# Row transform of the first layer on sums and differences of columns w and w+256, with strips split on GpSimd

## The reference

```python
# layer 0: a 3x3 convolution with complex weights, in the frequency plane
X = jnp.fft.rfftn(x, axes=(-2, -1)); Xr, Xi = jnp.real(X), jnp.imag(X)
Yr = _rconv(Xr, wr) - _rconv(Xi, wi) + b_real[:, None, None]
Yi = _rconv(Xr, wi) + _rconv(Xi, wr) + b_imag[:, None, None]
y = jnp.fft.irfftn(lax.complex(Yr, Yi), axes=(-2, -1))
# layer 1: u, v = halves of the channels; whole rows are kept or set to zero
left_gate = relu(sign(einsum('bkmd,bkd->bkm', u, v.sum(axis=2))))[..., None]
y = concatenate([left_gate * u, right_gate * v], axis=1)
# layers 2 and 3: plain 3x3 convolutions, 16 to 16 channels, zero padding 1
```

## Time and profile before

| | |
|---|---|
| median of 3 runs | 4616.99 us (4616.7 to 4618.75) |
| the profiled execution, own time | 4618.31 us |
| its span | 4616.5 us |
| TensorE clock granted, mean | 0.959 of full speed |
| busy share: PE, PEld, DVE, ACT, POOL | 92%, 50%, 60%, 57%, 0% |

### The profile page before, as it was taken

One profiled execution on the slowest core, in us unless ns is written; L12 is line 12 of the kernel. 1 busy time (PEld: TensorE's weight loads), 2 busy tenths in 40 slices (PEclk: granted clock), 3 DMA queues, 4 the chain that ended last, 5 costly groups with the idle time before them and its releaser, 6 DMA issues.

```text
span 4616.5 us, 172871 instructions
## 1 busy us (share of the span) xinstructions
PE 4235.7 (92%) x60064; PEld 2295.8 (50%) x60064; DVE 2761.5 (60%) x9972; ACT 2639.8 (57%) x7597; POOL 3.5 (0%) x22
## 2 busy tenths in 40 slices
PE   4999899989999899998999989999899989888785
PEld 1555435555455544555445543555436553455441
DVE  1777727775377744777257771776727775377730
ACT  4456665547555565555655566555565556544453
POOL 0000000000000000000000000000000000000000
PEclk8999899999999999999999999999899999999987
DMA  7444666647665576665656566564766647544476
GB/s 203 110 120 114 166 162 175 175 132 183 159 177 175 139 171 163 176 175 147 162 160 176 168 160 165 159 175 145 170 157 177 177 135 183 144 120 124 107 183 183
DMA packets 437852, 732.96 MB, mean 159 GB/s; under 512 B 42544, under 2 KB 109296, under 8 KB 437232
## 3 DMA queue, kind: packets, MB, share of 16 engines
q1 hardware_dynamic: 416112, 688.51, 54.2%
q10 hardware_dynamic: 21248, 37.76, 4.1%
HBM read 323.98 MB, written 134.22 MB: 99 GB/s over the span
## 4 chain that ended last, share of the span: by engine, by line
PE 85%; DMA 6%; DVE 3%; issue 3%; SPq 2%; ACT 1%; ACTq 0%; DVEq 0%
PE ps L1358 26%; PE ps L1276 20%; PE ps L1261 19%; PE ps L1269 6%; PE ps L1285 5%; PE ps L1135 5%; DMA shared<-x 3%; DMA out<-x 2%; PE ps L1383 1%; DMA x<-x 1%; PE ps L1208 1%; PE ps L1181 1%; PE ps L1182 0%; SPq L401 0%; DVE shared L911 0%
## 5 line engine op out<-in xcount | busy, mean ns | idle before, releaser
L1358 PE MATMUL ps<-x,conv_s 64*32 64x512 f32 x12288 | 1398.5, 610 | 88.8 <-DMA shared<-x 83.6
L1358 PE MATMUL ps<-shared,conv_s 64*32 64x512 f32 x12288 | 1407.1, 609 | 0.0
L645 ACT ACTIVATE x<-ps,vec 128x256 f32 (+1 forms) x1024 | 491.3, 496 | 998.1 <-PE ps L1276 998.1
L1276 PE MATMUL ps<-hil,shared 128*128 128x256 f32 x4096 | 993.6, 386 | 0.0
L1276 PEld LDWEIGHTS ps<-hil,shared 128*128 128x128 f32 x4096 | 740.4, 190 | 273.8 <-issue 194.1
L911 DVE SCALAR_TENSOR_TENSOR shared<-xin,trig 128x256 f32<-128x256 f32 x2048 | 822.2, 440 | 57.3
L1358 PEld LDWEIGHTS ps<-x,conv_s 64*32 64x32 f32 x12288 | 428.0, 108 | 646.1 <-issue 581.6
L720 ACT ACTIVATE x<-ps,vec 64x512 f32<-64x512 f32 (+1 forms) x768 | 526.3, 685 | 340.7 <-PE ps L1358 331.1
L1261 PE MATMUL ps<-shared 32*32 32x512 f32 x16384 | 657.9, 602 | 0.0
L923 DVE COPY vsb<-ps 128x512 f32<-128x512 f32 x512 | 329.9, 686 | 545.9 <-PE ps L1261 545.9
L1358 PEld LDWEIGHTS ps<-shared,conv_s 64*32 64x32 f32 x12288 | 501.4, 108 | 196.6 <-issue 157.4
(11 more groups left out here) (175 smaller groups left out, 3366.5 us busy)
## 6 DMA issues: line engine op xcount, KB each, us to landing
shared<-x SPq DMA_DIRECT2D x680, 256.0 KB, 4.8
xin<-x SPq DMA_DIRECT2D x512, 256.0 KB
out<-x SPq DMA_DIRECT2D x512, 256.0 KB
shared<-x SPq DMA_DIRECT2D x128, 768.0 KB, 7.0
shared<-x SPq DMA_DIRECT2D x496, 128.0 KB, 3.5
shared<-t_strip SPq DMA_DIRECT2D x512, 96.0 KB, 3.7
shared<-x ACTq DMA_DIRECT2D x128, 256.0 KB, 4.3
x<-x SPq DMA_DIRECT2D x64, 256.0 KB, 9.1
```

Source lines behind the costliest of these rows:

```text
L645: ins = nc.scalar.activation(split_in(strip_of(s))[:, q, :], split_in(ps[:, bank, :])[:, q, :], ACT.Identity, bias=v1(MEAN), accum_out=sum ...
L1276: mm = pe.matmul(split_in(ps[:, BY + 2 * odd + e, :])[:, int(q < 2), :], xt[:, e, q, :], hil[:, q, 0:HALF], start=False, stop=True, skip_g ...
L1358: mm = pe.matmul(ps[TM * cg:TM * cg + TM, banks[k], :], conv_s[rows, kw, kind, :], of, start=(kw == 0), stop=(kw == TAPS - 1), skip_group_ ...
```

## The change

Each strip of x is replaced, in place, by `low = x[w] + x[w+256] - 2 mean` and `high = x[w] - x[w+256]`. The Hilbert table has period 512 and couples only columns of opposite parity, so that sums give only sums and differences only differences: each of the four products of a strip now has 128 columns in place of 256. Cosine and sine change sign from w to w+256, so a plane's low half is made of differences and its high half of sums. Y stays in sums and differences in `x1` through the first layer (a factor 0.5 is folded into weights and tables), and is put together again by the gates.

The parts: (a) GpSimd splits each strip (three operations of 256 columns, each waiting for the one before), and DVE's planes wait for `x_split`, no more for the DMA; (b) a plane is two operations of 128 columns with sums and one of 256 without, and DVE's subtraction of the mean is gone; (c) `hilbert` has 128 columns; (d) `evict` is three activations; (e) the gates are two GpSimd operations of 128 columns (`lift`) and two DVE operations of 256 columns with two tensor inputs, with waits both ways; (f) V copies signal on two semaphores; (g) the small products over the same table are in three pieces where they were two; (h) six more small DVE operations in the preparation of the next image, two on the column sums, two ahead of the gates.

```diff
@@ gpsimd
+    pool.wait_ge(v_scaled, i + 1)
+    with pool.Fori(0, STRIPS // UNROLL) as j:
+        for k in range(UNROLL):
+            low, high = (halves(xin[:, k, :])[:, h, :] for h in range(2))
+            pool.wait_ge(x_loaded[k], (i * (STRIPS // UNROLL) + j + 1) * 16)
+            b.then(nc.gpsimd.tensor_tensor(high, low, high, ALU.subtract))
+            b.then(nc.gpsimd.tensor_scalar(low, low, v1(MEAN), 2.0, ALU.subtract, ALU.mult))
+            nc.gpsimd.tensor_tensor(low, low, high, ALU.subtract).then_inc(x_split, 1)
...
+    pool.wait_ge(v_gates, i + 1)
+    for n in range(STRIPS):
+        s = STRIPS - 1 - n
+        pool.wait_ge(gated, gd(i, n - LIFT_FREE + 1))
+        for q in range(2):
+            ins = nc.gpsimd.tensor_scalar(split_in(lifts[n % LIFT_FREE])[:, q, :], signs(x1[:, s, 1:1 + N])[:, 0, q, :], cols[:, 4, s:s + 1],
+                                          gate_b[:, q, s:s + 1], ALU.mult, ALU.add)
+        ins.then_inc(lifted, 1)
@@ scalar, evict
-        ins = nc.scalar.activation(split_in(strip_of(s))[:, q, :], split_in(ps[:, bank, :])[:, q, :], ACT.Identity, bias=v1(MEAN),
-                                   accum_out=sums[:, q, bass.ds(s, 1)])
-    ins.then_inc(y_evicted, 1)
+        nc.scalar.activation(signs(strip_of(s))[:, 0, q, :], signs(ps[:, bank, :])[:, 0, q, :], ACT.Identity, bias=v1(MEAN),
+                             accum_out=sums[:, q, bass.ds(s, 1)])
+    nc.scalar.activation(halves(strip_of(s))[:, 1, :], halves(ps[:, bank, :])[:, 1, :], ACT.Identity).then_inc(y_evicted, 1)
@@ vector, make_planes
-    dve.wait_ge(x_loaded[k], loads * 16)
+    dve.wait_ge(x_split, t0 + s + 1)
...
-    b.did(V.tensor_scalar(xin[:, k, :], xin[:, k, :], v1(MEAN), None, ALU.subtract))
...
+            b.did(V.scalar_tensor_tensor(signs(planes[:, a, k, :])[:, 0, q, :], signs(xin[:, k, :])[:, 1, q, :], 1.0, signs(trig[:, a, :])[:, 0, q, :],
+                                         ALU.mult, ALU.mult, accum_out=gsum[:, 2 * a + q, bass.ds(s, 1)]))
+        ins = V.tensor_tensor(halves(planes[:, a, k, :])[:, 1, :], halves(xin[:, k, :])[:, 0, :], halves(trig[:, a, :])[:, 0, :], ALU.mult)
@@ vector, gates
-            ins = V.tensor_scalar(of, of, cols[:, 4, bass.ds(s, 1)], gate_b[:, q, bass.ds(s, 1)], ALU.mult, ALU.add)
-        ins.then_inc(gated, 1)
+        dve.wait_ge(lifted, t0 + j * GROUP + k + 1)
+        V.scalar_tensor_tensor(low, high, cols[:, 4, bass.ds(s, 1)], lifts[k], ALU.mult, ALU.add).then_inc(low_gated, 1)
...
+        dve.wait_ge(low_gated, t0 + j * GROUP + k + 1)
+        V.scalar_tensor_tensor(high, high, cols[:, 5, bass.ds(s, 1)], lifts[k], ALU.mult, ALU.add).then_inc(gated, 1)
@@ tensor, hilbert
-        mm = pe.matmul(split_in(ps[:, BY + 2 * odd + e, :])[:, int(q < 2), :], xt[:, e, q, :], hil[:, q, 0:HALF],
+        mm = pe.matmul(signs(ps[:, BY + 2 * odd + e, :])[:, q % 2, int(q < 2), :], xt[:, e, q, :], hil_s[:, q, :],
```

More of the change, by code:

```diff
@@ L86, in tables @@
         cols = n[1::2] if k < 2 else n[::2]
-        hil_t[:, k, :HALF] = hil[rows][:, cols]
-        hil_t[:, k, HALF:] = g[rows]
+        if k % 2 == 0:
+            hil_t[:, HALF * (k // 2):HALF * (k // 2 + 1)] = hil[rows][:, cols]
+            for half, sign in enumerate((1, -1)):
+                hil_t[:, HIL_S + P * (k + half):HIL_S + P * (k + half + 1)] = hil[rows][:, cols[:P]] + sign * hil[rows][:, cols[P:]]
+        hil_t[:, HIL_G + NG * k:HIL_G + NG * (k + 1)] = g[rows]
     mean_fix = np.zeros((P, NG))
@@ L283, in program @@
         vc, vs, vy = (work[:, k, :] for k in range(3))
+        lifts = [a[:, HALF * h:HALF * (h + 1)] for a in (colv, vs) for h in range(2)]
+        junk_d = xt[:, 1].rearrange("p a b -> p (a b)")
         shifted = work[:].rearrange("p a w -> p (a w)")[:, 0:3 * KINDS * STRIPS].rearrange("p (j k s) -> p j k s", j=3, k=KINDS)
@@ L810, in _ @@
                 st.then(V.tensor_scalar(u[sl, :], br[sl, 0, :], bias_w[sl, 0:1], None, ALU.mult))
-                V.scalar_tensor_tensor(u[sl, :], br[sl, 1, :], bias_w[sl, 1:2], u[sl, :], ALU.mult, ALU.add).then_inc(s_based, 1)
+                st.then(V.scalar_tensor_tensor(u[sl, :], br[sl, 1, :], bias_w[sl, 1:2], u[sl, :], ALU.mult, ALU.add))
+                low, high = (halves(u[sl, :])[:, k, :] for k in range(2))
+                st.then(V.tensor_tensor(high, low, high, ALU.subtract))
+                V.scalar_tensor_tensor(low, low, 2.0, high, ALU.mult, ALU.subtract).then_inc(s_based, 1)
             dve.wait_ge(s_based, 2)
@@ L885, in prepare @@
                 c.settle()
+                low, high = (halves(u[0:48, :])[:, k, :] for k in range(2))
+                c.then(V.tensor_tensor(high, low, high, ALU.subtract))
+                c.then(V.scalar_tensor_tensor(low, low, 2.0, high, ALU.mult, ALU.subtract))
                 V.tensor_copy(u[HP:HP + 48, :], u[0:48, :]).then_inc(v_u, 1)
-                V.tensor_scalar(u_sum, u[2 * C:4 * C, :], small[2 * C:4 * C, 1:2], None, ALU.mult).then_inc(v_zc, 1)
+                c.then(V.tensor_scalar(u_sum, u[2 * C:4 * C, :], small[2 * C:4 * C, 1:2], None, ALU.mult))
+                low, high = (halves(u_sum)[:, k, :] for k in range(2))
+                c.then(V.tensor_tensor(high, low, high, ALU.subtract))
+                V.scalar_tensor_tensor(low, low, 2.0, high, ALU.mult, ALU.subtract).then_inc(v_zc, 1)
                 dve.wait_ge(v_u, n + 1)
@@ L946, in step @@
                             b = steps_of(s)
-                            make_planes(b, s, k, u0 + uses + 1, pair + 1)
+                            make_planes(b, s, k, pair + 1)
                             assert b.n == DVE_B, b.n
                         if e == 0:
-                            for f in range(2):
-                                copy_v(pair * 2 + f, f, pair)
+                            copy_v(pair)
                     if dotting:
@@ L963, in image @@
                 dve.wait_ge(a_cols, 6 * i + 6)
+                dve.sem_inc(s_dve, 1)
+                low, high = (halves(colv)[:, k, :] for k in range(2))
+                c.then(V.tensor_tensor(high, low, high, ALU.subtract))
+                c.then(V.scalar_tensor_tensor(low, low, 2.0, high, ALU.mult, ALU.subtract))
                 dve.sem_inc(s_dve, 1)
@@ L997, in image @@
                 w1, w2 = (work[:, k, 0:2 * STRIPS].rearrange("p (q s) -> p q s", q=2) for k in range(2))
+                c.then(V.tensor_scalar(sums[:], sums[:], 2.0, None, ALU.mult))
                 c.did(V.scalar_tensor_tensor(w1, edge[:], float(HALF), sums[:], ALU.mult, ALU.add))
@@ L1250, in mix @@
                     due()
-                    pe.wait_ge(v_copied, t0 + t * 2) if type(t) is not int or t > 0 else None
-                    due()
+                    for e in range(2):
+                        pe.wait_ge(v_copied[e], i * PAIRS + t) if type(t) is not int or t > 0 else None
+                        due()
                     for a in (AXS, AXB, AXC):
@@ L1378, in convolutions @@
                 due()
[L1379 removed]
+                pe.wait_ge(gated, gd(i, 1))
                 due()
```

127 lines of the change are left out of this document (77 added, 50 removed).

## The result

The changed kernel takes 4707.93 us (median of 4 runs, 4704.29 to 4709.5), the kernel before 4617.62 beside it: a ratio of 1.0194, 95% interval 1.0177 to 1.0212, so slower by just under 2% and clear of noise. The forecast was 4415.

A forecast was written before the change was run, and what follows sets the result against it. The prediction took TensorE to bound the kernel, with ACT close beside it in the first layer. Savings of 193 + 12 + 7 - 8 = 204 us from 4618.3 gave a forecast of 4415 us, range 4370 to 4460.

The forecast's parts named there:

- (c) The halved products: Hilbert products at 0.125 us each, 0.75 us less a strip; the second's saving mostly lost to a 0.7 us ACT wait.
- (b) The planes without GpSimd: DVE's planes in the first layer: 2.35 us a strip for 2.65; nothing in the loop, 7 us at layer starts.
- The model of the chain from load to transpose: First layer, load through split, planes and V copy to transpose: 10.05 us against a limit of 11.15.
- 193 + 12 + 7 = 212: First-layer savings in us: 193 from loop steps at 0.78 each, 12 from each layer's last two products, 7 from planes.
- the split's price (a): GpSimd's three split operations in the first layer: 1.9 us a strip, bounds 1.2 to 4.0, hidden up to 3.0.
- exclusion rival: GpSimd and DVE exclude each other, their times add: +87 us in the loop, +136 in the second convolution, 4830; chance 0.31.
- GpSimd is slow by itself: Rival: at 4.0 us a strip for the split the loop's gain is gone, 4660 us; chance 0.06.
- What would show it: Listed signs: lengthened DVE or POOL operations for exclusion; planes waiting for GpSimd while DVE idles for slow GpSimd.
- the gates (e): Second convolution: GpSimd's lifts 0.3 us each, 0.7 a strip with wait, under TensorE's 1.26; +0.5 us for the order.
- -8 us: Cost of the gates, small added operations and semaphores together, between 0 and -30 us.
- an estimate of 0.56 us: Skill's 2.6 cycles an element for two-input GpSimd operations: 0.56 us for 256 columns before dispatch, so the sum would stay.

The follow-up runs named there:

- a_neither: The changed kernel with GpSimd's three split operations and its two lifts a strip both left out: 4383.6 us.
- a_fast: The changed kernel with only the middle split operation rewritten as times 2 by a pointer, then plus a column of twice the mean negated: 4644.7 us.
- a_nogate: The changed kernel with DVE's two gate operations a strip left out, GpSimd's lifts and all signals kept: 4571.6 us.
- a_free: The changed kernel with GpSimd's three split operations made on an idle tile and DVE not waiting for them until the layer's end: 4529.0 us.

## Why the prediction was wrong

**Right.** (c) The halved products: 0.12 us each (569.4 us busy in place of 993.6), the second one's saving swallowed by ACT, with a wait of 0.64 where 0.7 was said. (b) The planes without GpSimd: 2.34 us, 2.35 taken. The model of the chain from load to transpose, with 11.15 us as its limit, held as well: 12.31 in the trace after, and a TensorE that waits 1.17 us for the V copy.

**Right in kind, too small.** The first layer without GpSimd's split is 252 us below before; the terms for it were 193 + 12 + 7 = 212. A step saves 0.91 us on average (10.15 to 9.24 in a_neither) and not 0.78: the first strip's products went from 1.83 us to 1.00, which is 0.83 by the prediction's own rows and not the 0.75 that it took for both strips; the second strip's gave 0.10, where 0.03 was taken. That is 31 of the 40 us; this error went in the kernel's favour and hid part of the ones that follow.

**Wrong, first: the split's price (a).** The step "I take 0.6 for the two operations with two inputs and 0.5 for the one between, 1.9 us a strip" failed. It stood on the row for a memset, which has no input, and was scaled by columns and streams; the kind of arithmetic, by which the same 256 columns take 0.55 or 1.15 us, no row could show. Measured: 0.85, 1.49, 0.81 and 0.3 of waits, 3.44. The prediction's bounds were 1.2 to 4.0, and even alone the three take 0.73 + 1.14 + 0.73 + 0.3 = 2.9. The planes behind it, 2.35 taken, last 3.08 (854.15 to 857.23) beside GpSimd. The limit of 3.0 us a strip that the prediction set stood on planes of 2.35; with 3.08 the same 11.15 leaves 2.3, and a_fast, at 3.01, still stands 120 us above a_neither. Price: 190 us. The prediction had an overlap wrong as well as a cost: it priced the hold only in its exclusion rival, as DVE's sum, and not in the chain. The rival "GpSimd is slow by itself" named half of this mechanism, with a chance of 0.06; of the signs listed under "What would show it", those of both rivals appeared.

**Wrong, second: the gates (e).** "I take 0.3, so 0.7 a strip with its wait" for GpSimd's lifts: they take 0.77 each and 1.54 a strip, above TensorE's 1.35. Price: 121 us in the convolution and 11 ahead of it. Alone a lift takes 0.45, which would have passed; the hold by DVE's gates makes the difference (a_nogate). The prediction put -8 us on all of this.

**The exclusion rival** forecast +87 us in the first layer's loop and 136 in the second convolution, 4830 in all. The second figure is near the 121 measured, by nearly its mechanism, but the engine that lacks time is GpSimd, not DVE. The first failed: DVE's lengthened operations cost 5 us by themselves (a_free), though they lengthen the chain. The Trainium skill (SBUF — State Buffer, section Who interferes with whom) has the second of such instructions wait for the whole of the first. The trace agrees: DVE's instruction from 850.19 is under way when GpSimd's starts at 850.20, which then lasts 1.26 us, 0.54 more than its shortest; DVE's next one, from 850.80, lasts 1.21, 0.53 more than the one before it. They take turns, each waiting for the other's instruction to end. What the rule doesn't say is whether that costs anything: it cost 5 us where nobody waited for GpSimd, and most of 121 where GpSimd had no slack. Of the Trainium skill, GPSIMD Engine Reference, section 3.1 (Elementwise — side-by-side cycle accounting), led to an estimate of 0.56 us for two inputs and 256 columns before dispatch; alone 0.73 was measured.

**A third term** was missed: from the edge products to the second convolution even a_neither takes 25 us more than before, 3 an image. Most of it is a pause within the 192 edge products. The groups before and in a_neither, the pause itself, and DVE's first operation on their result:

```profile
L1330 PE MATMUL ps<-work,mix_s 32*32 32x64 f32 x1536 | 17.0, 224 | 0.0
```

```profile
L1400 PE MATMUL ps<-work,mix_s 32*32 32x64 f32 x1536 | 18.8, 224 | 16.7 <-issue 16.7
...
1484.58 0.34 PE L1400 MATMUL ps<-work,mix_s 32*32 32x64 f32 x13 [1.87 <-issue]
...
1485.00 0.36 DVE L1035 TENSOR_SCALAR edge<-ps 128x64 f32<-128x64 f32 x2 [1.78 <-PE ps L1400]
```

From the first to the last edge product it takes 15.3 us over 8 images before, 33.7 in a_neither and 32.2 in the changed kernel: 18 of the 25 us, and 17 of the changed kernel's 36. The pause stands in every image of the changed kernel and of its 17 variants, behind the same product (the 179th in six images of eight), and in no image of the kernel before, though these products are the same in both. What TensorE waits for there the profile doesn't show, and nothing was tried on it; the cause stays open. The other 7 us of the 25 are what the added small operations and a lower clock may have cost. The windows before and in a_neither:

```profile
1560.00:1584.00 24.00, 11.08 (x186) 7.53 (x178) 17.99 (x83) 5.71 (x18) 0.31 (x2) 0.73 0.16 42
```

```profile
1481.00:1508.00 27.00, 13.69 (x234) 10.20 (x219) 19.85 (x88) 6.97 (x24) 0.31 (x2) 0.62 0.13 36
```

DVE has 1.9 us more work in it, and the granted clock is 0.62 on average in place of 0.73, closer to the lower of its two levels. How the 7 us divide between the two was not tried.

The terms against the forecast's 204 us: first layer 62 and not 212 (150 short), edges 36 and not 8 (28), second convolution 121 and not 0; together 299, and some 5 us gained elsewhere make the miss of 293.

## What to carry to other kernels

Work that goes to an idle engine isn't free when a result has to come back: add up the whole chain from the load to the first consumer with that engine's real prices, and where the trace has none, run one instruction of the exact form before deciding. Where the two engines also lengthen each other's operations, take the lengthened prices at every place of that chain. An operation's price on GpSimd depended here on its arithmetic by a factor of two, and again by up to two on what DVE did beside it; so for a rate take the price beside a busy DVE. Where two engines share the load, look for the balance: with none, one, two and four of four odd lifts on DVE the kernel took 4545.9, 4491.3, 4456.8 and 4498.8 us.

## What the runs showed of the hardware

On GpSimd, f32, 256 columns, at the shortest: two inputs 0.72 us; "less, then times" 1.15 (pointer and immediate) or 1.22 (two pointers); a subtraction by pointer alone 0.93; a multiplication by an immediate alone 0.86; "times, then plus" by two pointers 0.55, and 0.45 on 128 columns. Why the last is cheapest, no run shows. In the loop, beside DVE, the medians of the forms with 256 columns are, in the same order, 0.74 to 0.80, 1.36, 1.43, 1.14, 0.94 and 1.03, and single ones last over 2 us; DVE's own rise from 0.42 to 0.57 and from 0.69 to 0.84 on average.
